# Decoder layer on one core: in the attention stage, the sum of the two output halves, its split, the output projection and the residual addition move one step later, and the first group of transposes moves to directly behind the scores

## The chip, the cores and the metric

The kernel runs on one core of one Trainium2 chip. The metric is the device time of one execution in microseconds (us); lower is better. TensorE is called PE here, VectorE DVE, ScalarE ACT, GpSimd POOL and SyncE SP, as in the profile. Each of the five works through a queue of its own in program order, and the queues wait for each other only by semaphores that are written into the kernel by hand.

## The reference, cut to what matters

A pre-norm decoder layer on x of 4 x 512 x 512: causal attention with 32 query heads and 8 key/value heads of size 64, then a small cross attention, then a mixture of 8 experts. The change touches only the attention, which is:

```python
    q = _rope((x @ Wq.T).reshape(B, L, HQ, HD))      # B 4, L 512, HQ 32, HD 64
    k = _rope((x @ Wk.T).reshape(B, L, HKV, HD))     # HKV 8, so G = 4 query heads share one
    v = (x @ Wv.T).reshape(B, L, HKV, HD)
    attn = einsum('bkgqd,bkld->bkgql', qh, kh) * SCALE
    p = softmax(where(causal, attn, -inf), axis=-1)
    out = einsum('bkgql,bkld->bkgqd', p, vh)
    return out @ Wo.T                                # added to x
```

## The kernel before, in words

All operands of the matmuls are split into a high and a low part (`_hi`, `_lo`), each held in a reduced 32-bit type, and each product is two or three matmuls over these parts. ACT makes the high part with a copy (`act_split`), and DVE subtracts it from the source for the low part (`dve_lo`, line L422).

The attention walks over 8 groups (one key/value head each). In a group it walks over 16 steps `c`: 4 batches `b` times 4 heads `h`. A step is a slice of a software pipeline, and every engine has its own function that issues its part of step `c`: `pe_group`, `act_group`, `dve_group`, `pool_group`. The order of the calls in these four functions is the order of work; nothing else schedules it. Groups 1 to 6 are two trips through a loop with three groups in its body.

In step `c` head `n + 1` gets its scores on PE (L208, 8 matmuls), the causal mask and row maximum on DVE (`dve_masked`, L434), the exponential on ACT (`act_exp`, L313), reciprocals on DVE (`dve_recip`, L441) and its normalisation on POOL (`pool_norm`, L546). Head `d = c - 1` has its probabilities transposed on PE in three units (`pe_ptrans`, L218): unit 0 of 4 tiles, unit 1 of 4 tiles, and unit 2 of 2 tiles, which comes at the very start of the next step. Units 0 and 2 share one PSUM bank, unit 1 has another, so unit 0 of a head must wait until unit 2 of the head before was read by ACT (`pt_hi`, the copy) and DVE (`pt_lo`, the subtraction). Then head `d - 1` is multiplied with v (`pe_pv`, L235, 8 matmuls into the one bank `O_BANK`). Its result comes as two halves: ACT copies one to `o_part` (`act_opart`, tile `v_and_o`), DVE adds the other (`dve_oadd`, L487, tile `o_f`), which also frees `O_BANK` for the next `pe_pv`. After two heads the pair is split (`act_o` gives `o_hi`, `dve_o` gives `o_lo`). Once in a step PE projects one of the four row blocks of the last finished batch (`pe_wo`, L247, 6 matmuls), ACT copies this out (`act_wo`, L372), and POOL adds it to the residual (`pool_woacc`, L562).

Three of four steps also hold a projection for the next batch (`pe_proj`, L185, 12 matmuls): of v and k at h = 0, of queries at h = 1 and 2. At h = 3 there is none, only a small transpose of v (`pe_vt`, L195). I call h = 3 the short step. Rotary embedding of these takes DVE (`dve_rope_in`, L452 and L453), POOL (`pool_rope`, two operations, L537 and L539), ACT (`act_rope`) and DVE or POOL (`dve_q_lo`, L459 and L460; `pool_k_lo`, L554). Once in a group the next weights are split, too: `w2` by ACT and DVE, `w1` by ACT and POOL at `W1_SLOTS` (b = 2, h = 1, 2, 3).

Of the kernel before, what the change touches and what calls it, by code (L numbers as in the profile page):

```python
# [26 lines left out]
B, L, D = 4, 512, 512  # L27
# [71 lines left out]
def decoder_layer(nc, x, ctx, ctx_cols, mem_mask, wqkv, wo_rows, router_cols, router_b, gu_w, gu_b, down_w, down_b,  # L99
                  cos_t, sin_t, causal_t, ident_t, iota_t, out):  # L100
    stack = ExitStack()
    with stack:
# [149 lines left out]
        def pe_group(pe, g, r):  # L252
# [4 lines left out]
            for c in range(HEADS + (isinstance(g, int) and g == GROUPS - 1)):  # L257
# [9 lines left out]
                d_here = not (isinstance(g, int) and g == 0 and d < 0)  # L267
                d_begun = not (isinstance(g, int) and g == 0 and d < 1)
                d_last = not (isinstance(g, int) and g == 0 and db < 1)
                d_before_last = not (isinstance(g, int) and g == 0 and db < 2)  # L270
# [26 lines left out]
                if dh in (1, 2) and d_last:  # L297
                    if dh == 1 and db == 1:
                        pe.wait_ge(s["w2_lo_done"], 2 * g + 2)
                    pe_wo(pe, dm - 1, (db - 1) % 2, dh - 1)  # L300
                if dh == 0 and d_before_last:
                    pe_wo(pe, dm - 2, db % 2, 3)
# [71 lines left out]
        def act_group(act, g, r):  # L374

            for c in range(HEADS + (isinstance(g, int) and g == GROUPS - 1)):
# [9 lines left out]
                d_here = not (isinstance(g, int) and g == 0 and d < 0)  # L386
                d_begun = not (isinstance(g, int) and g == 0 and d < 1)
                d_last = not (isinstance(g, int) and g == 0 and db < 1)
                d_before_last = not (isinstance(g, int) and g == 0 and db < 2)
# [13 lines left out]
                if dh == 3 and d_last:  # L403
                    act_wo(act, dm - 1, 2)
                if h == 3 and next_batch:
                    act_v(act, m + 1, (b + 1) % 2)
                if d_begun:
                    act_opart(act, dn_ - 1)
                if dh in (1, 2) and d_last:
# [1260 lines left out]
```

## Time and profile before

| what | value |
|---|---|
| median of 3 runs | 1655.32 us (1653.87 to 1656.75) |
| profiled execution, its time and its span | 1654.71 us, 1653.0 us |
| busy share PE, DVE, ACT, POOL over the span | 90%, 80%, 67%, 63% |
| granted PE clock over 180 to 900 us | 1.00 |
| PE busy in 420 to 540 us | 112.66 of 120.00 us |
| DVE, ACT, POOL busy there | 98.44, 96.71, 98.39 us |

The attention takes from about 60 us to about 1065 us of the span; what follows is not changed. The profile's idle times stand in brackets behind an instruction, with what ended them.

### The profile page before, as it was taken

The numbers are of one execution on the slowest core, as the hardware profiler recorded it, in microseconds if no ns is written. First come the engines' busy times: TensorE is split into PE (matmuls) and PEld (weight loads), VectorE is DVE, ScalarE is ACT, GpSimd is POOL, SyncE is SP. The second block draws the span as 40 slices with busy tenths as digits, with TensorE's granted clock in tenths as the row PEclk, the third lists the DMA queues.
The fourth block names the chain that finished last, engine by engine and source line by source line (L and its number), as shares of the span: only waits on it lengthen the run. The fifth ranks groups of instructions, "written<-read, shape, count | busy, mean of one in ns | idle before, by whom it ended". The sixth has DMA issues, their size and how long they took to land. (4 is left out here: it accounts for less than half of the span.)

```text
span 1653.0 us, 31706 instructions
## 1 busy us (share of the span) xinstructions
PE 1487.3 (90%) x8951; PEld 1305.1 (79%) x8951; DVE 1329.5 (80%) x3470; ACT 1113.7 (67%) x2593; POOL 1049.0 (63%) x1161
## 2 busy tenths in 40 slices
PE   5799999999999999999999999698689999999994
PEld 4678888888888778878878877577479999999993
DVE  7688888888888888888888888388678998898892
ACT  3687887887887788788778878432156666666661
POOL 6668878878878878878878877556613223322321
PEclk9799999999999999999999999967589999999997
DMA  4000000000000000000000000112368878888775
GB/s 173 1 13 20 2 14 20 1 14 20 1 14 21 3 14 20 1 14 20 1 14 1 1 1 1 41 64 90 108 213 230 238 218 217 232 236 219 196 180 134
DMA packets 62033, 124.98 MB, mean 76 GB/s; under 512 B 20942, under 2 KB 21070, under 8 KB 61792
## 3 DMA queue, kind: packets, MB, share of 16 engines
q1 hardware_dynamic: 51408, 102.24, 19.5%
q0 software_dynamic: 10304, 20.59, 6.6%
q8 instruction: 77, 1.26, 0.3%
q14 instruction: 100, 0.82, 0.2%
q10 hardware_dynamic: 144, 0.07, 0.0%
HBM read 106.08 MB, written 24.71 MB: 79 GB/s over the span
## 5 line engine op out<-in xcount | busy, mean ns | idle before, releaser
L546 POOL TENSOR_SCALAR probs<-probs,row_inv 128x512 f32<-128x512 f32 (+3 forms) x512 | 303.6, 614 | 15.1 <-DVE row_inv L441 15.1
L313 ACT ACTIVATE probs<-probs,neg_max 128x512 f32<-128x512 f32 (+3 forms) x512 | 281.7, 552 | 28.5 <-DVE neg_max L434 25.6
L434 DVE CUSTOM_DVE_ANT_0 probs<-bank,causal 128x512 f32<-128x512 f32 (+3 forms) x512 | 220.5, 485 | 54.6 <-PE bank L208 53.7
L1246 POOL DMA_INDIRECT acc<-ctx_raw,idx x46 | 74.6, 1621 | 294.3 <-ACT ctx_raw L1399 280.0
L218 PE MATMUL bank<-ident,probs 128*128 128x128 f32 x1280 | 185.0, 275 | 60.1 <-DVE pt_lo L422 55.7
L422 DVE TENSOR_TENSOR pt_lo<-bank,pt_hi 128x512 fp32r<-128x512 f32 (+1 forms) x384 | 216.3, 591 | 26.2 <-ACT pt_hi L306 26.2
L218 PEld LDWEIGHTS bank<-ident,probs 128*128 128x128 f32 x1280 | 149.7, 141 | 96.8 <-DVE pt_lo L422 58.8
L537 POOL TENSOR_TENSOR rot<-rot,sin 128x512 f32<-128x512 f32 (+1 forms) x96 | 123.6, 1287 | 156.2 <-DVE rot L453 151.7
L1327 PE MATMUL bank<-xt_hi,gu_hi 128*128 128x256 f32 x736 | 208.1, 283 | 2.0 <-DVE xt_lo L422 1.5
L1327 PE MATMUL bank<-xt_hi,gu_lo 128*128 128x256 f32 x736 | 206.3, 280 | 0.0
L1327 PE MATMUL bank<-xt_lo,gu_hi 128*128 128x256 f32 x736 | 206.3, 280 | 0.0
L306 ACT ACTIVATE pt_hi<-bank 128x512 fp32r<-128x512 f32 (+1 forms) x384 | 184.9, 515 | 29.8 <-PE bank L218 26.7
L562 POOL TENSOR_TENSOR x_res<-wo_out,x_res 128x512 f32<-128x512 f32 x128 | 168.6, 1317 | 24.6 <-ACT wo_out L372 24.3
L208 PE MATMUL bank<-k_hi,q_st 128*128 128x256 f32 (+2 forms) x512 | 173.4, 349 | 2.7 <-DVE xn_lo L422 2.7
L235 PE MATMUL bank<-pt_hi,v_st 128*128 128x256 f32 (+2 forms) x512 | 170.5, 344 | 1.5 <-DVE pt_lo L422 1.5
L208 PE MATMUL bank<-k_lo,q_st 128*128 128x256 f32 (+2 forms) x512 | 157.4, 329 | 0.0
L235 PE MATMUL bank<-pt_lo,v_st 128*128 128x256 f32 (+2 forms) x512 | 155.0, 325 | 0.0
L185 PE MATMUL bank<-xn_hi,w_hi 128*128 128x512 f32 x384 | 152.8, 398 | 0.2 <-DVE rot L453 0.2
L185 PE MATMUL bank<-xn_lo,w_hi 128*128 128x512 f32 x384 | 151.5, 394 | 0.0
L185 PE MATMUL bank<-xn_hi,w_lo 128*128 128x512 f32 x384 | 151.1, 394 | 0.0
L1327 PEld LDWEIGHTS bank<-xt_hi,gu_hi 128*128 128x128 f32 x736 | 138.9, 189 | 6.0 <-issue 2.8
L1327 PEld LDWEIGHTS bank<-xt_lo,gu_hi 128*128 128x128 f32 x736 | 139.2, 189 | 3.0
(203 smaller groups left out, 4077.4 us busy)
## 6 DMA issues: line engine op xcount, KB each, us to landing
gu_raw<-in_gate_up SPq DMA_DIRECT2D x92, 512.0 KB, 4.2
dn_raw<-in_down SPq DMA_DIRECT2D x92, 256.0 KB, 3.7
w_raw<-in_wqkv SPq DMA_DIRECT2D x8, 768.0 KB, 4.5
w_raw<-in_wo_rows SPq DMA_DIRECT2D x8, 512.0 KB, 3.6
h_rows<-ln_h SPq DMA_DIRECT2D x16, 256.0 KB, 2.0
acc<-x_res SPq DMA_DIRECT2D x4, 1024.0 KB, 4.8
x_res<-in_x SPq DMA_DIRECT2D x3, 1024.0 KB, 11.3
ctx_raw<-in_ctx SPq DMA_DIRECT2D x2, 512.0 KB, 6.5
```

The source lines that it names most:

```text
L185: last = nc.tensor.matmul(PJ_BANK[:, :], w1[sp][:, c, r * P:(r + 1) * P], xn[mp][:, c, b * L:(b + 1) * L], start=first, stop=(c == DC - 1 ...
L208: last = nc.tensor.matmul(S_BANK[k][:, at:at + cols], q_st[:, h, i * P:(i + 1) * P], kk[:, kb, 0:cols], start=(a == 0), stop=(a == 1))
L218: last = nc.tensor.transpose(T_BANK[u % 2][:, k * P:(k + 1) * P], probs[:, hb, P_AT[i] + j * P:P_AT[i] + (j + 1) * P], ident[:, :])
L235: last = nc.tensor.matmul(dst, v_st[:, vb, j, :], rhs, start=(j == 0 and a == 0), stop=(j == QB - 1 and a == 1))
L306: nc.scalar.activation(dst, src, ACT.Copy).then_inc(sem_, 1)
L313: nc.scalar.activation(row, row, ACT.Exp, bias=neg_max[:, hb, i:i + 1], scale=-1.0, accum_out=row_sum[:, hb, i:i + 1]).then_inc(s["exp_don ...
L422: nc.vector.tensor_tensor(dst, src, hi.bitcast(F32), ALU.subtract).then_inc(sem_, 1)
L434: nc.vector.tensor_tensor_reduce(out=probs[:, hb, P_AT[i]:P_AT[i] + (i + 1) * P], in0=S_BANK[k][:, at:at + (i + 1) * P], in1=causal[:, (QB ...
L537: nc.gpsimd.tensor_tensor(rot[0:rows, :], rot[0:rows, :], sin[0:rows, :], ALU.mult).then_inc(s["rot_sin"], 1)
L546: nc.gpsimd.tensor_scalar(row, row, row_inv[:, hb, i:i + 1], 0.0, ALU.mult, ALU.add).then_inc(s["pnorm_done"], 1)
L562: nc.gpsimd.tensor_tensor(tile, wo_out[:, t % 2, :], tile, ALU.add).then_inc(s["woacc_done"], 1)
L1327: last = nc.tensor.matmul(GU_BANK[u % 3][:, side * TILE:(side + 1) * TILE], gu[sp_][:, ib, c, side, :], xts[mp][:, k, c, :], start=first, ...
```

## The change

`f = c - 2` is new. The sum of output halves, the split of the pair, the split of `w2`, the output projection, its copy and the residual addition now go by `f` where they went by `d = c - 1`: each is done for a head or a row block one step later. Unit 0 of the transposes, its copy and its subtraction are cut off from unit 1 and put directly behind the scores on PE. On ACT the order is now unit 2, output half, unit 0, then rotary and exponential; on DVE it is unit 2, split of the pair, sum, then the mask, then unit 0. The last group has one step more, and the tail behind it is shorter by that.

```diff
@@ pe_group
                 if more:
                     pe_scores(pe, n + 1, m if h < G - 1 else m + 1, (h + 1) % G, (b + (h == G - 1)) % 2)
+                if d_here:
+                    pe_ptrans(pe, dn_, (r + d) % 3, 0)
...
-                if dh == 3 and d_last:
-                    pe_wo(pe, dm - 1, (db - 1) % 2, 2)
+                if fh == 3 and f_last:
+                    pe_wo(pe, fm - 1, (fb - 1) % 2, 2)
                 if d_here:
-                    pe_ptrans(pe, dn_, (r + d) % 3, 0)
                     pe_ptrans(pe, dn_, (r + d) % 3, 1)
@@ act_group
                 if d_begun:
                     act_pt(act, dn_ - 1, (d + 1) % 2, 2)
+                if f_begun:
+                    act_opart(act, fn - 1)
+                if d_here:
+                    act_pt(act, dn_, d % 2, 0)
...
+                if f_begun and fh % 2 == 0:
+                    act_o(act, fn - 1, fm if fh else fm - 1, (f // 2 - 1) % 4)
                 if d_here:
-                    act_pt(act, dn_, d % 2, 0)
                     act_pt(act, dn_, d % 2, 1)
@@ dve_group
+                if d_begun:
+                    dve_pt(dve, dn_ - 1, (d + 1) % 2, 2)
+                if f_begun and fh % 2 == 1 and not (isinstance(g, int) and g == 0 and f == 1):
+                    dve_o(dve, HEADS // 2 * g + (f - 1) // 2 - 1, ((f - 1) // 2 - 1) % 4)
+                if f_begun:
+                    dve_oadd(dve, fn - 1, (f - 1) % 2, HEADS // 2 * g + (f - 1) // 2)
+                if fh == 1 and fb == 1:
+                    dve_w2(dve, g)
                 if more:
                     dve_masked(dve, n + 1, (r + c + 1) % 3)
-                if d_begun:
-                    dve_pt(dve, dn_ - 1, (d + 1) % 2, 2)
...
+                if d_here:
+                    dve_pt(dve, dn_, d % 2, 0)
...
                 if d_here:
-                    dve_pt(dve, dn_, d % 2, 0)
                     dve_pt(dve, dn_, d % 2, 1)
                 if h == 3 and next_batch:
                     dve_v(dve, m + 1, (b + 1) % 2)
-                if d_begun:
-                    dve_oadd(dve, dn_ - 1, (d - 1) % 2, HEADS // 2 * g + (d - 1) // 2)
```

DVE, the short step (h = 3), before: `pt1_lo` with 256 columns is unit 2, and the two `pt0_lo` are units 0 and 1 of the next head.

```order
L434 ISA probs,neg_max<-bank0,causal 128x512
L434 ISA neg_max 128x1
L434 ISA probs,neg_max<-bank1,causal 128x384
L434 ISA neg_max 128x1
L434 ISA probs,neg_max<-bank2,causal 128x256
L434 ISA neg_max 128x1
L434 ISA probs,neg_max<-bank2,causal 128x128
L434 ISA neg_max 128x1
L422 TENSOR_TENSOR pt1_lo<-bank3,pt1_hi 128x256
L441 RECIPROCAL row_inv<-row_sum 128x4
L422 TENSOR_TENSOR pt0_lo<-bank3,pt0_hi 128x512
L422 TENSOR_TENSOR pt0_lo<-bank4,pt0_hi 128x512
```

DVE, the same step after (lines are 10 higher there).

```order
L432 TENSOR_TENSOR pt0_lo<-bank3,pt0_hi 128x256
L432 TENSOR_TENSOR o_lo<-o_f,o_hi 128x512
L497 TENSOR_TENSOR o_f<-bank5,v_and_o 64x512
L444 ISA probs,neg_max<-bank0,causal 128x512
L444 ISA neg_max 128x1
L444 ISA probs,neg_max<-bank1,causal 128x384
L444 ISA neg_max 128x1
L444 ISA probs,neg_max<-bank2,causal 128x256
L444 ISA neg_max 128x1
L444 ISA probs,neg_max<-bank2,causal 128x128
L444 ISA neg_max 128x1
L432 TENSOR_TENSOR pt1_lo<-bank3,pt1_hi 128x512
```

Unit 2 is now ahead of the mask and not behind it, and so are a split of the pair (every second step, h = 1 and 3) and the sum of halves.

ACT, the short step, after; before, it went unit 2 (`pt_hi` with 256 columns), the four exponentials, units 0 and 1, `v_st`, `v_and_o`, `wo_out`, `o_hi`.

```order
L311 ACTIVATE pt1_hi<-bank3 128x256
L311 ACTIVATE v_and_o<-bank5 64x512
L311 ACTIVATE pt0_hi<-bank3 128x512
L318 ACTIVATE probs,row_sum<-probs,neg_max 128x512
L318 ACTIVATE probs,row_sum<-probs,neg_max 128x384
L318 ACTIVATE probs,row_sum<-probs,neg_max 128x256
L318 ACTIVATE probs,row_sum<-probs,neg_max 128x128
L311 ACTIVATE pt0_hi<-bank4 128x512
L311 ACTIVATE v_st<-bank6 128x4x64
L377 ACTIVATE wo_out<-bank7 128x512
```

The copy of the output half and of unit 0 went ahead of the exponentials; `o_hi` left this step for an even one.

PE, the short step, after: before, the 4 transposes between scores and L195 stood behind L195, in one run of 8.

```order
L218 MATMUL bank<-ident,probs 128x128 x2
L208 MATMUL bank<-k_hi,q_st 128x512
L208 MATMUL bank<-k_lo,q_st 128x512
L208 MATMUL bank<-k_hi,q_st 128x384
L208 MATMUL bank<-k_lo,q_st 128x384
L208 MATMUL bank<-k_hi,q_st 128x256
L208 MATMUL bank<-k_lo,q_st 128x256
L208 MATMUL bank<-k_hi,q_st 128x256
L208 MATMUL bank<-k_lo,q_st 128x256
L218 MATMUL bank<-ident,probs 128x128 x4
L195 MATMUL bank<-ident,v_and_o 128x64 x4
L218 MATMUL bank<-ident,probs 128x128 x4
```

In the three other steps the first x4 stands between the scores and the 12 matmuls of the projection.

## Rows read from the trace of the kernel before

**Rows 1.** Busy by stretch: one group, one plain batch, one with a further wait

```profile
core 0: us, PE busy (x) PEld busy (x) DVE busy (x) ACT busy (x) POOL busy (x), PEclk, DMA share, GB/s
513.52:546.09 32.57, 29.59 (x168) 25.35 (x168) 27.13 (x68) 25.12 (x65) 28.62 (x33) 1.00 0.08 25
420.84:450.94 30.10, 29.05 (x168) 25.36 (x168) 24.72 (x68) 24.59 (x64) 24.82 (x29) 1.00 0.01 2
388.25:513.52 125.27, 117.38 (x672) 101.44 (x672) 103.66 (x274) 100.94 (x255) 103.58 (x116) 1.00 0.04 12
```

**Rows 2.** Who waited for whom on PE, 180 to 1000 us

```profile
PE bank L218 <- DVE pt_lo L422: 39.0, 43, 1.6
```

**Rows 3.** Order of time on PE, a short step and the step behind it

```profile
447.83 0.38 PE L218 MATMUL bank<-ident,probs 128*128 128x128 f32 x2
447.97 0.47 PE L208 MATMUL bank<-k_hi,q_st 128*128 128x512 f32 x1
448.28 0.39 PE L208 MATMUL bank<-k_lo,q_st 128*128 128x512 f32 x1
...
449.43 0.46 PE L195 MATMUL bank<-ident,v_and_o 64*128 64x64 f32 x4
450.94 1.09 PE L218 MATMUL bank<-ident,probs 128*128 128x128 f32 x8 [1.05 <-DVE pt_lo L422]
451.79 0.48 PE L235 MATMUL bank<-pt_hi,v_st 128*128 128x512 f32 x1
...
453.17 0.40 PE L247 MATMUL bank<-w_hi,o_hi 128*128 128x512 f32 x1
...
454.55 0.38 PE L218 MATMUL bank<-ident,probs 128*128 128x128 f32 x2
...
456.06 0.40 PE L185 MATMUL bank<-xn_hi,w_hi 128*128 128x512 f32 x1
...
458.79 0.39 PE L247 MATMUL bank<-w_hi,o_hi 128*128 128x512 f32 x1
...
460.15 1.03 PE L218 MATMUL bank<-ident,probs 128*128 128x128 f32 x8
460.94 0.48 PE L235 MATMUL bank<-pt_hi,v_st 128*128 128x512 f32 x1
```

**Rows 4.** Order of time on DVE, the same steps

```profile
448.82 0.69 DVE L434 CUSTOM_DVE_ANT_0 probs<-bank,causal 128x512 f32<-128x512 f32 x1
...
450.47 0.42 DVE L422 TENSOR_TENSOR pt_lo<-bank,pt_hi 128x256 fp32r<-128x256 f32 x1
...
454.01 0.68 DVE L487 TENSOR_TENSOR o_f<-bank,v_and_o 64x512 f32<-64x512 f32 x1
...
457.52 0.68 DVE L422 TENSOR_TENSOR o_lo<-o_f,o_hi 128x512 fp32r<-128x512 f32 x1
```

**Rows 5.** Order of time on ACT, the same short step

```profile
448.11 0.60 ACT L372 ACTIVATE wo_out<-bank 128x512 f32<-128x512 f32 x1 [0.33 <-PE bank L247]
448.60 0.38 ACT L306 ACTIVATE pt_hi<-bank 128x256 fp32r<-128x256 f32 x1
449.55 0.72 ACT L313 ACTIVATE probs<-probs,neg_max 128x512 f32<-128x512 f32 x1 [0.57 <-DVE neg_max L434]
...
451.75 1.06 ACT L306 ACTIVATE pt_hi<-bank 128x512 fp32r<-128x512 f32 x2
452.70 0.37 ACT L306 ACTIVATE v_st<-bank 128x256 fp32r<-128x256 f32 x1
```

**Rows 6.** Order of time on POOL and DVE: same short step, and near 520 us

```profile
447.05 1.29 POOL L537 TENSOR_TENSOR rot<-rot,sin 128x512 f32<-128x512 f32 x1
448.42 1.29 POOL L539 TENSOR_TENSOR rope<-rope,rot 128x512 f32<-128x512 f32 x1
...
520.07 1.31 POOL L562 TENSOR_TENSOR x_res<-wo_out,x_res 128x512 f32<-128x512 f32 x1
520.10 3.07 DVE L422 TENSOR_TENSOR o_lo<-o_f,o_hi 128x512 fp32r<-128x512 f32 x1
521.32 1.31 POOL L469 TENSOR_TENSOR w_lo<-w_raw,w_hi 128x512 fp32r<-128x512 f32 x1
```

More of the change, by code:

```diff
@@ L252, in pe_group @@
         def pe_group(pe, g, r):
-            for c in range(HEADS + (isinstance(g, int) and g == GROUPS - 1)):
+            for c in range(HEADS + (2 if isinstance(g, int) and g == GROUPS - 1 else 0)):
                 b, h = divmod(c, G)
@@ L266, in pe_group @@
                 dn_, dm = HEADS * g + d, B * g + db
-                d_here = not (isinstance(g, int) and g == 0 and d < 0)
+                d_here = not (isinstance(g, int) and g == 0 and d < 0) and d < HEADS
                 d_begun = not (isinstance(g, int) and g == 0 and d < 1)
-                d_last = not (isinstance(g, int) and g == 0 and db < 1)
-                d_before_last = not (isinstance(g, int) and g == 0 and db < 2)
+                f = c - 2
+                fb, fh = divmod(f, G)
+                fn, fm = HEADS * g + f, B * g + fb
+                f_begun = not (isinstance(g, int) and g == 0 and f < 1)
+                f_last = not (isinstance(g, int) and g == 0 and fb < 1)
+                f_before_last = not (isinstance(g, int) and g == 0 and fb < 2)
                 if d_begun:
@@ L296, in pe_group @@
                     pe_pv(pe, dn_ - 1, dm if dh else dm - 1, (d + 1) % 2, (db if dh else db + 1) % 2)
[L297 to L298 removed]
+                if fh in (1, 2) and f_last:
+                    if fh == 1 and fb == 1:
                         pe.wait_ge(s["w2_lo_done"], 2 * g + 2)
[L300 to L302 removed]
+                    pe_wo(pe, fm - 1, (fb - 1) % 2, fh - 1)
+                if fh == 0 and f_before_last:
+                    pe_wo(pe, fm - 2, fb % 2, 3)
         def act_split(dst, src, sem_):
@@ L374, in act_group @@
         def act_group(act, g, r):
-            for c in range(HEADS + (isinstance(g, int) and g == GROUPS - 1)):
+            for c in range(HEADS + (2 if isinstance(g, int) and g == GROUPS - 1 else 0)):
                 b, h = divmod(c, G)
@@ L493, in dve_group @@
         def dve_group(dve, g, r):
-            for c in range(HEADS + (isinstance(g, int) and g == GROUPS - 1)):
+            for c in range(HEADS + (2 if isinstance(g, int) and g == GROUPS - 1 else 0)):
                 b, h = divmod(c, G)
@@ L518, in dve_group @@
                     dve_q_lo(dve, m + 1, 1, (b + 1) % 2)
-                if dh == 1 and db == 1:
-                    dve_w2(dve, g)
                 if h < 3 and next_batch:
@@ L551, in pool_k_lo @@
             wait(pool, s["pnorm_done"], 16 * m - 8)
-            wait(pool, s["woacc_done"], 4 * m - 9)
+            wait(pool, s["woacc_done"], 4 * m - 10)
             for half_ in range(2):
@@ L564, in pool_group @@
         def pool_group(pool, g, r):
-            for c in range(HEADS + (isinstance(g, int) and g == GROUPS - 1)):
+            for c in range(HEADS + (2 if isinstance(g, int) and g == GROUPS - 1 else 0)):
                 b, h = divmod(c, G)
@@ L575, in pool_group @@
                 dn_, dm = HEADS * g + d, B * g + db
-                d_here = not (isinstance(g, int) and g == 0 and d < 0)
+                d_here = not (isinstance(g, int) and g == 0 and d < 0) and d < HEADS
                 d_begun = not (isinstance(g, int) and g == 0 and d < 1)
-                d_last = not (isinstance(g, int) and g == 0 and db < 1)
-                d_before_last = not (isinstance(g, int) and g == 0 and db < 2)
+                f = c - 2
+                fb, fh = divmod(f, G)
+                fn, fm = HEADS * g + f, B * g + fb
+                f_begun = not (isinstance(g, int) and g == 0 and f < 1)
+                f_last = not (isinstance(g, int) and g == 0 and fb < 1)
+                f_before_last = not (isinstance(g, int) and g == 0 and fb < 2)
                 if h == 1 and next_batch:
```

53 lines of the change are left out of this document (26 added, 27 removed).

## The prediction

> **What bounds the kernel now.** I read the page first, then busy time by stretch, then the list of waits, then the order of time on each engine. In the attention PE is the bound, but not wholly. A group of 16 steps takes 125.27 us, with PE busy for 117.38 and DVE, ACT and POOL for 101 to 104 each [rows 1]. So PE stands idle for 7.9 us in a group, 63 us in eight; more than that the change can't win. Between 180 and 1000 us PE waited 39.0 us, in 43 waits, for the low part of the transposed probabilities [rows 2].
>
> In the short step that wait is 1.05 us: the transposes of L218 start at 450.94 [rows 3]. DVE did the mask first, from 448.82, and unit 2 behind it, from 450.47 for 0.42 us, so PE's bank came free at 450.89 [rows 4]. A plain batch of four steps has this one wait and takes 30.10 us. Two of the four batches of a group have a further one: one takes 32.57 us, and by subtraction from 125.27 the other some 32.5 [rows 1]. One of these comes from a split of the pair, o_lo, that took 3.07 us in place of 0.68, since it was issued while POOL ran two two-input operations back to back, from 520.07 to 522.63, and ended 0.54 us behind them [rows 4, 6]. The other is PE at `pe_wo` behind the split of w2.
>
> **The price list, from one plain batch.** PE: unit 2 to first score 0.14; scores to the next kind 1.38 (1.46 to L195, less a gap); 8 transposes 0.79 without a wait; PV 1.38 (451.79 to 453.17); wo 1.38; projection 2.73 [rows 3]. ACT: the copy of wo starts 0.28 behind unit 2's start on PE, unit 2's copy 0.49 behind that and takes 0.38; four exponentials 2.20 (449.55 to 451.75); one 512-column copy 0.48 to 0.53; v follows, the next thing 0.30 later [rows 5]. DVE: mask 1.65 (448.82 to 450.47), its first tile lets ACT start 0.73 later (449.55); sum of halves 0.68; o_lo 0.68 [rows 4, 5]. A semaphore costs about 0.05 between ACT, DVE and PE.
>
> **The change, part by part.** No matmul, copy or subtraction is added or taken away. The sum, its split, wo and POOL's residual keep their lengths; moving wo by a step costs PE nothing, as it is still one per step. The extra step at the end holds what was in the tail: 0, with an estimate of 1 us either way for the steps without projections around it.
>
> Cutting the run of 8 transposes in two adds a switch from transposes back to matmuls in the three long steps. The first score follows unit 2 and takes 0.31 to the second (447.97 to 448.28), where matmuls of the same size in the projection take 2.73 / 12 = 0.23. So a switch costs 0.08, and three cost 0.24 per batch [rows 3]. Bounds: 0 and 0.24.
>
> Now the queues by hand, t from unit 2's start on PE, first the short step. PE is through its scores at 1.52. ACT copies wo at 0.28, unit 2 at 0.77 to 1.15; DVE subtracts from 1.20 to 1.62; unit 0 can start at 1.67: a wait of 0.15 in place of 1.05. That is the gain, 0.90 per batch. The same 0.15 comes up at h = 1, where nothing waited before; not at h = 2, since at h = 1 wo is earlier.
>
> What is late next: DVE has o_lo and the sum ahead of the mask. o_lo is issued at about 1.54. Before, POOL ran its rotary pair in the short step from 447.05 to 449.71, t = -0.78 to 1.88 [rows 6]. In the new order DVE's rotary work in the step before is later (the sum, unit 0 and the q subtractions are ahead of it), and I put the pair's end at t = 2.15. Held until there, o_lo ends at 2.15 + 0.54 = 2.69, the sum at 3.35, and PV, which needs the sum because of the one bank for its output, starts at 3.40. PE would be ready at 1.67 + 0.40 + 0.43 + 0.40 = 2.90. That is a new wait of 0.50. Bounds: 0 if o_lo isn't held (sum by 2.85), 0.5 as here. The Trainium skill, in its page "GPSIMD Engine Reference", section "Key points", says that GpSimd shares its SBUF interfaces with VectorE and contends with DVE instructions with two SBUF inputs; o_lo is one. The 3.07 us row agrees. By the rule the wait stands for any overlap, by the row for two-input POOL operations; both give my sum here.
>
> The mask then starts at 3.30 and not at 1.0 (448.82 - 447.83). ACT begins the exponentials at 4.03, ends them at 6.23, copies unit 1 until 6.75 and v until 7.05, and only then wo. PE's next step starts at 2.90 + 0.50 + 1.38 + 1.38 = 6.16, so wo's copy is at t = 0.9 of the next step and not at 0.28; unit 2's copy at 1.4, DVE done at 2.2, unit 0 at 2.27. PE waits 0.75 there. Before, no wait stood in this place, since the exponentials ran 2 us earlier. In the step h = 0 ACT catches up: its work is some 7.2 us, the step 8.5. In long steps the late mask is hidden behind the rotary copies on ACT and 2.73 us of projection.
>
> Sum of a plain batch: 30.10 - 1.05 - about 0.2 of restart behind the stall + 0.24 (switches) + 0.15 + 0.15 + 0.50 + 0.75 = 30.64, so +0.54.
>
> The batch with w2: ACT splits w2 (two copies, 1.04) ahead of unit 2 in the short step, so unit 0 waits 1.2 and not 0.15; but PV's wait goes, since the sum is then hidden behind it. DVE does both w2 subtractions (0.7 to 0.87 each) ahead of the mask; wo waits 0.2 for them, and the wait of the next step grows from 0.75 to 2.1. I get +2.1 over a plain batch, against 2.4 before. The batch with w1: POOL's extra operation pushes the rotary pair and ACT's copies come 0.5 ahead of unit 2 at h = 3 and h = 0: short step 7.24 and not 6.2, the next one +0.5, together +1.5 against 2.4 before, as the 3.07 us of o_lo are gone.
>
> Group: 4 x 0.54 - 0.3 - 0.9 = +0.96; times 8 = +7.7. From the profiled execution's 1654.71: **1662 us**, which stands 0.4% above it and above the median of 1655.32.
>
> **The rivals.**
> (a) Forecast: the short step's wait is traded for a PV wait there and a late unit 0 in the next; slower by 4 to 16 us, 1658 to 1670 (per group 0.5 to 2, by the bounds of the switches and of the hold). Chance 0.40.
> (b) ACT keeps up, and o_lo gets in ahead of POOL: then no PV wait (0.50 less), and the lag of 0.75 in the next step shrinks to about 0.3: -0.95 per batch against (a), 4 x 8 x 0.95 = 30 us less, 1632. With one of the two alone about 1640 to 1648. For it: DVE, ACT and POOL have 21 to 24 us of slack in a group. Against: the chain unit 2, o_lo, sum, mask, exponentials, unit 1, v, wo is 6.9 us long, and the short step on PE only 5.7. Chance 0.30. This is the one on the other side; it decides when wo's copy in step h = 0 starts before t = 0.5.
> (c) The q subtractions, now behind the mask and unit 0 (t = 4.4 to 6.1 at h = 2), fall on POOL's residual addition, a two-input operation of 1.3 us, and are held. By my walk they miss it by 0.2 us. If held, the rotary pair is 1.2 later, falls wholly on o_lo in the short step, and PV waits 1.2 more: up to 4 x 8 x 1.2 = 38 us on top, 1700; in part of the batches 1680. The Trainium skill's sentence on shared interfaces speaks for it; the row of 3.07 shows its size. Chance 0.18.
> (d) Nothing to be measured: gains of the two special batches cancel the plain ones, 1652 to 1658. Chance 0.12.
>
> **How the numbers follow.** About 0.2% (3.3 us) is what a measurement of this kernel can tell from no change. Faster is (b) with the lower edge of (d) and a part of (a)'s misjudged terms: 0.32. Same: 0.14, from (d) and (a)'s lower edge. Slower: 0.54, from (a) and (c). The range leaves out 0.1 on each side: from 1638, which holds most of (b), to 1688, which holds the partial case of (c). The likeliest case's own range is 1658 to 1670.
>
> **What the profile after would show.** Right: L218 (x4) behind the scores waits about 0.15 in the short step and at h = 1; PV (L235) waits some 0.5 in the short step for the sum; L218 waits about 0.75 at h = 0 for DVE; a plain batch takes 30.6 us, a group 126.2; o_lo at 128x512 has about 1.2 us as its usual length; the mask starts 3.3 us into the short step, and ACT waits there for it. Wrong would be: wo's copy at h = 0 directly behind PE; o_lo at 0.68 throughout (b); q_st rows near 1.5 to 2 us at h = 2 (c); PE busy near 118 of 120 us. My walk rests on differences of 0.1 to 0.3 us in where POOL's pair falls, and that is what would most likely make it wrong.

## The result, and the profile after

The changed kernel takes 1656.39 us (median of 20 runs, 1652.97 to 1662.57), the kernel before 1654.58 us (20 runs, 1651.89 to 1657.19). Each ratio below is against the runs of before that were made along with the kernel; their medians lie between 1654.58 and 1655.33. Here the ratio is 1.0014 with a 95% interval of 1.0008 to 1.0021. That is 1.8 us slower. The interval leaves out 1, so the loss is real, but it is about half of the 3.3 us that the prediction took as the least to be told from no change, and a quarter of the 7.7 us forecast. In the profiled executions the last matmul of the attention ends at 1065.03 us and before at 1063.72, so 1.3 us are lost there; the rest of the program, which is the same, took 591.07 against 589.28.

Busy time by stretch in the changed kernel, from one L195 to the next: the batch with w1, a plain batch, the two batches over which the split of w2 is spread, a group. It answers to [rows 1].

```profile
core 0: us, PE busy (x) PEld busy (x) DVE busy (x) ACT busy (x) POOL busy (x), PEclk, DMA share, GB/s
385.54:416.99 31.45, 29.84 (x170) 25.38 (x169) 26.06 (x69) 25.34 (x63) 27.87 (x31) 1.00 0.08 26
416.99:447.39 30.40, 29.67 (x169) 25.38 (x169) 26.13 (x68) 24.83 (x62) 25.36 (x29) 1.00 0.01 2
447.39:478.77 31.38, 29.66 (x170) 25.39 (x169) 26.10 (x68) 25.87 (x64) 26.43 (x30) 1.00 0.00 1
478.77:511.20 32.43, 30.03 (x170) 25.36 (x169) 27.35 (x71) 25.76 (x64) 26.40 (x29) 1.00 0.06 18
385.54:511.20 125.66, 119.21 (x674) 101.50 (x673) 105.64 (x275) 101.80 (x253) 106.07 (x116) 1.00 0.04 12
```

The plain batch went from 30.10 to 30.40 us, the group from 125.27 to 125.66. PE idles less (0.73 us in the plain batch, 1.05 before), yet the batch is longer: PE is busy for 29.67 us where it was for 29.05. A group before had two plain batches, now it has one: w2 is split one step later, so its first wait on PE stands ahead of an L195 and its others behind it. That first wait, in the short step, is 1.33 us:

```profile
478.18 0.66 PE L218 MATMUL bank<-ident,probs 128*128 128x128 f32 x4 [1.33 <-DVE pt_lo L432]
```

The list of waits on PE between 180 and 1000 us, against [rows 2], has more and shorter waits of about the same sum:

```profile
PE bank L218 <- DVE pt_lo L432: 41.0, 56, 1.7
```

PE in order of time, the short step and the scores of the step behind it (the same place of the program as [rows 3]):

```profile
444.79 0.38 PE L218 MATMUL bank<-ident,probs 128*128 128x128 f32 x2
...
446.80 0.66 PE L218 MATMUL bank<-ident,probs 128*128 128x128 f32 x4 [0.34 <-DVE pt_lo L432]
...
447.78 0.65 PE L218 MATMUL bank<-ident,probs 128*128 128x128 f32 x4
448.28 0.47 PE L235 MATMUL bank<-pt_hi,v_st 128*128 128x512 f32 x1
...
451.03 0.38 PE L218 MATMUL bank<-ident,probs 128*128 128x128 f32 x2
...
453.09 0.66 PE L218 MATMUL bank<-ident,probs 128*128 128x128 f32 x4 [0.39 <-DVE pt_lo L432]
453.50 0.48 PE L185 MATMUL bank<-xn_hi,w_hi 128*128 128x512 f32 x1
...
456.35 0.60 PE L218 MATMUL bank<-ident,probs 128*128 128x128 f32 x4
```

The wait of 1.05 has become 0.34 in the short step and 0.39 at h = 0. PV (L235) at 448.28 has no wait at all. DVE and POOL there, to hold against [rows 4, 6]:

```profile
446.67 0.68 DVE L432 TENSOR_TENSOR o_lo<-o_f,o_hi 128x512 fp32r<-128x512 f32 x1
447.45 0.68 DVE L497 TENSOR_TENSOR o_f<-bank,v_and_o 64x512 f32<-64x512 f32 x1
448.06 0.67 DVE L444 CUSTOM_DVE_ANT_0 probs<-bank,causal 128x512 f32<-128x512 f32 x1
...
445.31 1.30 POOL L552 TENSOR_TENSOR rot<-rot,sin 128x512 f32<-128x512 f32 x1 [0.32 <-DVE rot L463]
446.69 1.79 POOL L554 TENSOR_TENSOR rope<-rope,rot 128x512 f32<-128x512 f32 x1
```

POOL's pair lies at t = 0.52 to 3.69 from unit 2's start at 444.79, right on o_lo, as feared. But between its two operations POOL is free for 0.08 us (446.61 to 446.69), and o_lo starts in just this gap: it takes 0.68, and POOL's addition 1.79 in place of 1.29. In the plain batch's other split, at h = 1, o_lo does start beside a running POOL addition (430.50) and takes 1.68, but no wait on PE follows from it. ACT, against [rows 5]:

```profile
445.45 0.58 ACT L377 ACTIVATE wo_out<-bank 128x512 f32<-128x512 f32 x1
445.92 0.37 ACT L311 ACTIVATE pt_hi<-bank 128x256 fp32r<-128x256 f32 x1
...
451.72 0.58 ACT L377 ACTIVATE wo_out<-bank 128x512 f32<-128x512 f32 x1
```

The copy of wo comes 0.66 behind unit 2 in the short step, where it came at 0.28, and 0.69 at h = 0.

**A ring without PE.** What sets the 30.40? Follow the other engines through a plain batch:

```profile
428.84 1.29 POOL L552 TENSOR_TENSOR rot<-rot,sin 64x512 f32<-64x512 f32 x1 [4.17 <-DVE rot L463]
...
433.99 1.29 POOL L577 TENSOR_TENSOR x_res<-wo_out,x_res 128x512 f32<-128x512 f32 x1
435.36 2.65 POOL L569 TENSOR_TENSOR k_lo<-rope,k_hi 64x512 fp32r<-64x512 f32 x2
438.17 1.29 POOL L552 TENSOR_TENSOR rot<-rot,sin 128x512 f32<-128x512 f32 x1 [0.16 <-POOL k_lo L569]
439.53 1.29 POOL L554 TENSOR_TENSOR rope<-rope,rot 128x512 f32<-128x512 f32 x1
...
459.15 1.29 POOL L552 TENSOR_TENSOR rot<-rot,sin 64x512 f32<-64x512 f32 x1 [4.08 <-DVE rot L463]
```

POOL works without a pause of more than 0.2 us from 428.84 to 440.80. ACT waits for its end to make the high part of the queries (440.94), then does exponentials, `o_hi`, unit 1, wo (445.45) and unit 2. DVE goes on with unit 2, o_lo, sum and mask (448.06). ACT waits for the mask, then does its exponentials, unit 1, v, wo and unit 2 (to 452.58) and `o_part`. DVE waits for `o_part`, then does sum, mask, unit 0, the subtractions of the queries and the rotary input, and with that releases POOL at 459.15. One turn is 459.15 - 428.84 = 30.31 us, the length of the batch; at each link the instruction starts on the end of the one named before it, and none of them is a wait for PE. So I had a second theory, that this ring, and not PE, sets the plain batch.

### The profile page after: what moved, and what is told of

Same layout as the page of the kernel before. It is cut to its first block and busy times, and to the rows that moved or that the text cites. A ratio compares the mean times of both kernels' runs of the same rounds, so it can differ in the third digit from the quotient of the medians.

```text
span 1656.1 us, 31706 instructions
## 1 busy us (share of the span) xinstructions
PE 1502.3 (91%) x8951; PEld 1307.8 (79%) x8951; DVE 1345.6 (81%) x3470; ACT 1119.9 (68%) x2593; POOL 1070.5 (65%) x1161
## 5 line engine op out<-in xcount | busy, mean ns | idle before, releaser
L432 DVE TENSOR_TENSOR pt_lo<-bank,pt_hi 128x512 fp32r<-128x512 f32 (+1 forms) x384 | 229.8, 599 | 87.5 <-ACT pt_hi L311 79.8
L311 ACT ACTIVATE pt_hi<-bank 128x512 fp32r<-128x512 f32 (+1 forms) x384 | 199.6, 521 | 98.5 <-PE bank L218 96.9
L218 PE MATMUL bank<-ident,probs 128*128 128x128 f32 x1280 | 208.5, 278 | 58.2 <-DVE pt_lo L432 56.6
L218 PEld LDWEIGHTS bank<-ident,probs 128*128 128x128 f32 x1280 | 150.0, 140 | 104.1 <-DVE pt_lo L432 52.4
L577 POOL TENSOR_TENSOR x_res<-wo_out,x_res 128x512 f32<-128x512 f32 x128 | 178.7, 1396 | 14.9 <-ACT wo_out L377 14.6
L235 PE MATMUL bank<-pt_hi,v_st 128*128 128x256 f32 (+2 forms) x512 | 172.1, 347 | 2.0 <-DVE o_f L497 1.9
L185 PE MATMUL bank<-xn_hi,w_hi 128*128 128x512 f32 x384 | 161.2, 420 | 0.3 <-DVE rot L463 0.3
L235 PE MATMUL bank<-pt_lo,v_st 128*128 128x256 f32 (+2 forms) x512 | 156.7, 327 | 0.0
```

The source lines that it names most:

```text
L185: last = nc.tensor.matmul(PJ_BANK[:, :], w1[sp][:, c, r * P:(r + 1) * P], xn[mp][:, c, b * L:(b + 1) * L], start=first, stop=(c == DC - 1 ...
L218: last = nc.tensor.transpose(T_BANK[u % 2][:, k * P:(k + 1) * P], probs[:, hb, P_AT[i] + j * P:P_AT[i] + (j + 1) * P], ident[:, :])
L235: last = nc.tensor.matmul(dst, v_st[:, vb, j, :], rhs, start=(j == 0 and a == 0), stop=(j == QB - 1 and a == 1))
L311: nc.scalar.activation(dst, src, ACT.Copy).then_inc(sem_, 1)
L432: nc.vector.tensor_tensor(dst, src, hi.bitcast(F32), ALU.subtract).then_inc(sem_, 1)
L577: nc.gpsimd.tensor_tensor(tile, wo_out[:, t % 2, :], tile, ALU.add).then_inc(s["woacc_done"], 1)
```

## The experiments

All changes are against the changed kernel where nothing else is said. "Plain" is the plain batch from one L195 to the next, "end" the end of the last L247, "rest" the span behind it; these three are of the profiled execution. "wo" is the output projection, "residual" POOL's residual addition.

| kernel | median us | ratio to before, 95% | plain | end | rest |
|---|---|---|---|---|---|
| before | 1654.58 | 1 | 30.12 | 1063.72 | 589.28 |
| after | 1656.39 | 1.0014 [1.0008, 1.0021] | 30.40 | 1065.03 | 591.07 |
| x1 unit 0 early alone, on before | 1717.38 | 1.0389 [1.0366, 1.0411] | 32.24 | 1123.82 | 590.18 |
| x2 unit 0 early at h = 3 only | 1674.77 | 1.0126 [1.0106, 1.0146] | 30.96 | 1079.47 | 588.83 |
| x3 split of the pair earlier | 1658.21 | 1.0024 [1.001, 1.0038] | 29.95 | 1063.74 | 592.16 |
| x4 copy of wo behind unit 2 | 1655.51 | 1.0002 [0.9991, 1.0014] | 30.38 | 1061.97 | 593.73 |
| x5 residual later | 1652.06 | 0.9984 [0.9975, 0.9992] | 30.21 | 1058.75 | 591.95 |
| x6 extra POOL work in the ring | 1700.31 | 1.0275 [1.0259, 1.029] | 31.50 | 1108.59 | 591.01 |
| x7 the same outside of it | 1663.11 | 1.0058 [1.0045, 1.0071] | 30.39 | 1069.86 | 588.84 |
| x8 o_lo a little later | 1661.63 | 1.0052 [1.0037, 1.0067] | 30.39 or 31.52 | 1066.66 | 591.64 |
| x9 shift by a step alone | 1681.42 | 1.0158 [1.0143, 1.0172] | 31.53 | 1086.87 | 591.13 |
| x10 x9 and residual later | 1673.07 | 1.0103 [1.0088, 1.0119] | 30.96 | 1080.55 | 591.65 |
| x11 x3 and x5 | 1655.01 | 0.9994 [0.9983, 1.0005] | 29.82 | 1059.34 | 594.36 |
| x12 x3, x4 and x5 | 1642.79 | 0.9919 [0.9906, 0.9931] | 29.81 | 1053.13 | 589.67 |

### The failing term: is o_lo held, and what does that cost?

**x8.** A small memset stands ahead of the split in the short step, to push it out of the gap.

```diff
+                if h == 3 and next_batch:
+                    nc.vector.memset(tiny[:, 0:16], 0.0)
                 if f_begun and fh % 2 == 1 and not (...):
                     dve_o(dve, ...)
```

> The changed kernel with a small memset on VectorE (128x16) ahead of the subtraction that makes the low half of the output (o_lo) in the step h=3, so that this subtraction comes some 0.06 us or more later and misses the gap of 0.08 us between GpSimd's rotary product and addition. Theory hold (a two-input subtraction of VectorE that starts beside a running two-input op of GpSimd is held to its end): o_lo takes 1.5 to 2.4 us instead of 0.68 in each batch, the PV matmuls of the short step wait or the ring gets longer by 0.8 to 1.3 us, total 1675 to 1700 us, as far as the forecast of 1662 and beyond. Rival (no hold, or the hold is hidden there): o_lo 0.7 to 0.9 us or hidden, total 1654 to 1660 us.

Of the seven short steps in front of a plain batch between 160 and 930 us, three have o_lo at 1.77 or 1.78 us, and their batches take 31.43 to 31.52 us; the other four have it at 0.67. Two of these places in the trace of x8, in the first o_lo held, in the second not (DVE, POOL, and PE's PV):

```profile
417.09 1.77 DVE L433 TENSOR_TENSOR o_lo<-o_f,o_hi 128x512 fp32r<-128x512 f32 x1
417.05 1.26 POOL L557 TENSOR_TENSOR rope<-rope,rot 128x512 f32<-128x512 f32 x1
419.80 0.47 PE L236 MATMUL bank<-pt_hi,v_st 128*128 128x512 f32 x1 [0.95 <-DVE o_f L498]
...
543.84 0.67 DVE L433 TENSOR_TENSOR o_lo<-o_f,o_hi 128x512 fp32r<-128x512 f32 x1
543.83 1.81 POOL L557 TENSOR_TENSOR rope<-rope,rot 128x512 f32<-128x512 f32 x1
545.44 0.47 PE L236 MATMUL bank<-pt_hi,v_st 128*128 128x512 f32 x1
```

And the stretches, the first with o_lo held at its start, the second with o_lo not held:

```profile
417.80:449.32 31.52, 29.83 (x170) 25.40 (x169) 27.22 (x70) 24.82 (x62) 25.25 (x29) 1.00 0.01 2
672.84:703.23 30.39, 29.68 (x169) 25.39 (x169) 26.14 (x69) 24.81 (x62) 25.37 (x29) 1.00 0.01 2
```

The hold exists, it makes PV wait 0.95 us, and it lengthens the batch by 1.13 us. Where DVE's operation starts 0.04 us after POOL's, DVE pays 1.1; where the two start within 0.02, POOL pays 0.5. The step between the two is sharp: of all short steps in x8, o_lo at 0.03 us behind POOL's start was held and at 0.023 not.

How long a held o_lo lasts follows from POOL's operation. In the 14 traces between 160 and 1050 us, a POOL operation was already running at the start of o_lo 584 times. In 558 of these o_lo ended 0.53 to 0.72 us behind that operation's end, be it a TENSOR_TENSOR or a TENSOR_SCALAR; in 24 a further POOL operation followed at once and came first too, as in the 3.07 us of [rows 6]. If all eight plain batches were held, 8 x 1.13 = 9 us would come on top of 1656.4, an estimate of 1665. The expected 1675 and more was too much: in only three of the seven places did the small memset move o_lo far enough to be held.

### The two parts of the change apart

**x1.** Only unit 0 is moved to directly behind the scores, on all engines, and DVE's unit 2 ahead of the mask; the sum, its split and wo stay in their step.

```diff
@@ on the kernel before; pe_group, act_group and dve_group alike
                 if more:
                     pe_scores(...)
+                if d_here:
+                    pe_ptrans(pe, dn_, (r + d) % 3, 0)
...
-                    pe_ptrans(pe, dn_, (r + d) % 3, 0)
                     pe_ptrans(pe, dn_, (r + d) % 3, 1)
```

> The kernel before, with only one part of the change: unit 0 directly behind the scores on all three engines and unit 2 ahead of the mask on DVE; sum, split, projection and residual where they were. My theory: the short step's wait falls from 1.05 to about 0.3 us, but in each other step unit 0 now has only the 1.4 us of scores to hide copy and subtraction of unit 2, with wo_out (and every second step o_hi) ahead of them on ACT, so it waits 0.15 at h = 1 and about 0.7 at h = 0 and h = 2, and the switches cost 0.24: a plain batch about 30.8 us (30.10 before), in all 1660 to 1675 us. Rival, the transposes alone bring the gain and the shift by one step is what costs it: a plain batch below 29.6 us, 1640 us or less. Rival, PE's waits are only moved since another engine bounds the batch: 1655 us within 3.

It is far slower than any theory had it. In its plain batch PE waits for unit 0 in each of the four steps, 2.34 us together, most at h = 0, where ACT first waits for the sum to make `o_hi` and only then copies unit 2:

```profile
445.90 0.63 ACT L307 ACTIVATE o_hi<-o_f 128x512 fp32r<-128x512 f32 x1 [0.30 <-DVE o_f L489]
...
447.31 0.66 PE L218 MATMUL bank<-ident,probs 128*128 128x128 f32 x4 [1.35 <-DVE pt_lo L424]
```

**x9.** The other part alone: the shift by one step, with unit 0 beside unit 1 and DVE's mask ahead of unit 2, as before.

```diff
@@ dve_group; pe_group and act_group have unit 0 back beside unit 1 too
+                if more:
+                    dve_masked(dve, n + 1, (r + c + 1) % 3)
                 if d_begun:
                     dve_pt(dve, dn_ - 1, (d + 1) % 2, 2)
...
-                if more:
-                    dve_masked(dve, n + 1, (r + c + 1) % 3)
-                if d_here:
-                    dve_pt(dve, dn_, d % 2, 0)
```

> Only one part of the change: the sum of the output halves, its split, the projection and the residual one step later as in the changed kernel, but unit 0 of the transposes beside unit 1 as before, on all engines, and VectorE's mask ahead of the subtraction of unit 2. With it the two parts and their sum are known: transposes alone gave 1717, both 1656. Theory parts that need each other: the shift alone takes o_hi and the sum off the chain of the short step and costs no switches (TensorE's work 29.06 us in a plain batch as before), but GpSimd, ScalarE and VectorE close their ring, so the plain batch is 29.6 to 30.4 us, total 1640 to 1660 us. Rival (the shift is the harmful part that the early unit mends): plain batch over 31 us, total over 1670 us.

The rival's numbers came, 1681 us and 31.53 us. Its short step, on DVE and PE:

```profile
455.04 0.42 DVE L432 TENSOR_TENSOR pt_lo<-bank,pt_hi 128x256 fp32r<-128x256 f32 x1
...
456.16 0.68 DVE L497 TENSOR_TENSOR o_f<-bank,v_and_o 64x512 f32<-64x512 f32 x1
...
455.51 1.09 PE L218 MATMUL bank<-ident,probs 128*128 128x128 f32 x8 [1.05 <-DVE pt_lo L432]
456.99 0.47 PE L235 MATMUL bank<-pt_hi,v_st 128*128 128x512 f32 x1 [0.38 <-DVE o_f L497]
```

The old wait of 1.05 stays, since unit 2 still stands behind the mask, and the sum, now behind unit 2, brings the PV wait that I had forecast for the whole change. The two waits are 1.43 of the batch's 31.53 us, where before it was 1.05 of 30.12; most of the rest is PE's busy time, 29.91 where it was 29.06, though no switch between kinds of matmul was added. So each part alone costs (+62 and +26 us on the medians), and together they cost 1.8: by the rows, the shift takes the sum off the chain to unit 0, and the early unit 2 takes the mask off the chain to the sum.

x9 has one more thing to show, at h = 1 (DVE, then POOL):

```profile
439.20 2.04 DVE L432 TENSOR_TENSOR o_lo<-o_f,o_hi 128x512 fp32r<-128x512 f32 x1
...
437.36 2.07 POOL L561 TENSOR_SCALAR probs<-probs,row_inv 128x512 f32<-128x512 f32 x4
439.38 1.31 POOL L577 TENSOR_TENSOR x_res<-wo_out,x_res 128x512 f32<-128x512 f32 x1
```

Here o_lo starts 0.18 us ahead of POOL's addition and is held all the same, to 0.55 us behind the addition's end, and so it is in 18 places of this trace. POOL's normalisation was still running when o_lo started. Being ahead of the next POOL operation is not enough; POOL has to be idle.

**x2.** Unit 0 early only at h = 3, where the wait was; beside unit 1 elsewhere, which saves the switches.

```diff
-                if d_here:
+                if d_here and h == 3:
                     pe_ptrans(pe, dn_, (r + d) % 3, 0)
...
+                if d_here and h != 3:
+                    pe_ptrans(pe, dn_, (r + d) % 3, 0)
```

> The changed kernel with unit 0 early in the short step alone; in the three long steps it goes back to unit 1 on PE, ACT and DVE. My theory: the waits of 0.39 at h = 0 and those at h = 1 vanish behind the projection, and so do three switches of 0.08, so a plain batch takes 29.5 to 29.7 us (30.40 in the changed kernel, 30.10 before), in all about 1630 us (1625 to 1640). Rival, unit 0 early in the long steps is what keeps ACT and DVE on time, or these two bound the batch: no gain, 1652 to 1660 us, with the wait moved to unit 2 or PV.

A miss: 18 us slower than the changed kernel. In the long steps ACT and DVE now treat unit 0 behind the late exponentials, and unit 2 of the following step needs the same bank:

```profile
434.19 0.44 PE L218 MATMUL bank<-ident,probs 128*128 128x128 f32 x2 [0.51 <-DVE pt_lo L436]
```

The waits of this kind before and behind it are 0.72 and 0.70. The switches that x2 saves are worth less; how little stands in the part on why the prediction was wrong.

### Is there a ring?

**x6 and x7.** One more POOL addition of 128x480 elements per batch, whose result nobody reads: in x6 between k_lo and the rotary product of h = 1, in x7 at the end of h = 3.

```diff
@@ x6
                 if h == 1 and next_batch:
                     pool_k_lo(pool, m + 1, (b + 1) % 2)
+                    nc.gpsimd.tensor_tensor(spare[:, :], cos[:, 0:480], sin[:, 0:480], ALU.add)
@@ x7, behind pool_woacc
+                if h == 3 and next_batch:
+                    nc.gpsimd.tensor_tensor(spare[:, :], cos[:, 0:480], sin[:, 0:480], ALU.add)
```

> The changed kernel with an added GpSimd addition of 128x480 elements from two inputs (about 1.2 us by the durations of the neighbouring ones) in h=1 of each batch, between k_lo and the second rotary product. Nothing reads its result. Theory ring: it lies in the ring, so each of 32 batches takes 1.2 us longer, total +35 to +42 us, about 1691 to 1699 us. Rival (ring not closed; TensorE's side sets the batch): the op falls in time that GpSimd waits anyway later in the batch, total +0 to +10 us.

> The same added GpSimd addition of 128x480 elements, but at the end of h=3 of each batch, in front of GpSimd's wait of 4 us for the next rotary input. Theory ring: there GpSimd has slack, total unchanged within 3 us (1654 to 1660 us). A theory by which GpSimd's busy share sets the batch expects +35 to +42 us, as in the other place.

x6, POOL's new operation, then the plain batch:

```profile
450.56 1.22 POOL L603 TENSOR_TENSOR spare<-cos,sin 128x480 bf16<-128x480 f32 x1
...
429.47:460.97 31.50, 29.84 (x169) 25.42 (x168) 26.12 (x68) 24.82 (x62) 26.53 (x30) 1.00 0.01 2
```

x7, the batch with w1 and a plain batch:

```profile
386.82:419.40 32.58, 30.09 (x170) 25.45 (x169) 27.36 (x69) 25.32 (x63) 29.01 (x32) 1.00 0.08 25
419.40:449.79 30.39, 29.66 (x169) 25.37 (x168) 26.13 (x68) 24.80 (x62) 26.55 (x30) 1.00 0.01 2
```

The same operation lengthens the plain batch by 1.10 us in one place and not at all in the other: POOL's load is equal in both (26.53 and 26.55), so it is the place that counts. One turn of POOL's rotary work is now 31.42 us (441.31 to 472.73), 1.11 more. The two runs show that the place is on the path that closes the batch; that no wait for PE lies on this path rests on the rows. x6 costs 44 us in all and not 35: most batches, not only the plain ones, grew by about 1.1 us, and five grew by 2.2 to 3.4.

In x7 only the batch with w1 grew (32.58 from L195 to L195, 31.45 without the operation). There `w_lo` follows at once, and the subtraction of the queries is issued beside the two, in DVE's and POOL's order of time:

```profile
396.40 2.46 DVE L470 TENSOR_TENSOR q_st<-rope,q_st 64x512 fp32r<-64x512 f32 x1
...
395.85 1.22 POOL L611 TENSOR_TENSOR spare<-cos,sin 128x480 bf16<-128x480 f32 x1
397.03 1.29 POOL L480 TENSOR_TENSOR w_lo<-w_raw,w_hi 128x512 fp32r<-128x512 f32 x1
```

It is held to the end of both, 2.46 us in place of 1.28 in the changed kernel, which is the whole growth. This is the mechanism of rival (c), with its price, in a place where it can happen.

**x5.** One POOL residual addition out of the ring.

```diff
@@ pool_group, behind pool_rope
+                if h == 1:
+                    e = c - 3
+                    eb, em = e // G, B * g + e // G
+                    if not (isinstance(g, int) and g == 0 and eb < 1):
+                        pool_woacc(pool, em - 1, (eb - 1) % B, 1)
...
-                if fh and f_last:
+                if fh and f_last and h != 0:
```

> The changed kernel with one edit: GpSimd's residual addition that stood at the end of the step h=0 (1.37 us) is moved behind the second rotary addition of h=1, so it no longer stands between the norm of h=0 and the subtraction for k_lo. Theory ring (the plain batch of 30.4 us is closed by a chain of GpSimd, ScalarE and VectorE instructions in which TensorE does not take part): the ring loses 1.37 us, the plain batch goes from 30.40 to 29.3 to 29.7 us, where TensorE's own work stops it (its waits in a plain batch are about 1 us together), TensorE's waits nearly vanish, total 1625 to 1640 us. Rival (the transposes and their subtractions on TensorE's side set the batch): plain batch 30.4 as before, total 1654 to 1659 us.

The direction is right and the size wrong: 4.3 us faster than the changed kernel, where 16 and more were expected. In its plain batch PE is busy for nearly all of the time:

```profile
412.73:442.94 30.21, 29.73 (x169) 25.38 (x168) 26.36 (x69) 24.92 (x62) 25.39 (x29) 1.00 0.01 2
```

With the ring 1.3 us shorter the batch loses 0.19 us and meets the next bound, PE's own 29.7 us with one wait of 0.38. Both limits lay within 0.2 us of each other in the plain batch.

**x3 and x4.** x3 moves the split of the pair one step earlier, ahead of unit 1's subtraction, so that o_lo leaves the ring; x4 moves ACT's copy of wo behind the copy of unit 2 in the step after it.

```diff
@@ x3, dve_group
-                if f_begun and fh % 2 == 1 and not (...):
-                    dve_o(dve, HEADS // 2 * g + (f - 1) // 2 - 1, ...)
...
+                if f_begun and fh % 2 == 0:
+                    dve_o(dve, HEADS // 2 * g + f // 2 - 1, (f // 2 - 1) % 4)
                 if d_here:
                     dve_pt(dve, dn_, d % 2, 1)
@@ x4, act_group, behind unit 2
+                if eh and not (isinstance(g, int) and g == 0 and eb < 1):
+                    act_wo(act, em - 1, eh - 1)
```

> The changed kernel with the low part of the output pair (o_lo) made one step earlier, in the step in which ACT makes o_hi, ahead of the subtraction of unit 1, so that it no longer stands ahead of the mask in the short step. My theory, the mask that comes late by o_lo and the sum is what makes ACT late at h = 0: the mask starts 0.6 us earlier in the short step, the wait at h = 0 (0.39) goes, that of unit 0 in the short step grows by about 0.15, a plain batch 30.0 to 30.1 us, in all 1643 to 1648 us. Rival, ACT is late for its own work and not for the mask: the wait at h = 0 stays, 1655 us within 3.

> The changed kernel with ACT's copy of the projected rows (wo_out) behind the copy of unit 2 of the next step and not ahead of it; POOL's residual addition follows it. My theory, unit 0 waits for a chain wo_out copy, unit 2 copy, subtraction that is longer than the scores: it becomes 0.3 to 0.5 us shorter in every step, the waits of unit 0 at h = 3 and h = 0 (0.34 and 0.39) nearly vanish in plain batches, a plain batch about 29.6 to 29.9 us, in all 1630 to 1640 us. Rival, the wait follows from the late exponentials and the order of the two copies changes nothing: 30.3 us, 1655 us within 3.

Both missed the expected totals, and both fit the ring: x3 takes an instruction out of it (plain 29.95), x4 only exchanges two of its links (30.38), and PE's waits there are 0.55 and 0.29. That fit is an argument from one number each; what the gain in x3's plain batch is given back to in its total was not followed.

**x10.** The edit of x5 on x9.

> The shift alone as in x9, and GpSimd's residual addition of h=0 moved behind the second rotary addition of h=1 as in x5. Theory ring: if the ring bounds x9, this takes up to 1.4 us off each plain batch, down to TensorE's own work plus small waits, 29.2 to 29.8 us, total 1625 to 1648 us. Rival (TensorE waits for the unit that is transposed last in the short step, as in the kernel before): no change against x9 within 0.3 us a batch.

The plain batch falls from 31.53 to 30.96 and the total by 8 us. That is more than the 0.3 us of the rival and far less than the ring theory gave, so in x9 both the ring and PE's waits take part; it was not resolved further.

### Towards a faster version

**x11** joins x3 and x5, **x12** joins x3, x4 and x5.

> The changed kernel with the residual addition later (x5: plain batch 30.21) and VectorE's split of the output one step earlier (x3: 29.95). Theory: the two act on different things, the ring and the wait of unit 0, so the plain batch is 29.7 to 29.9 us, close to TensorE's own work of some 29.4 to 29.7; the attention ends 6 to 9 us earlier than in the changed kernel, of which 1 to 5 us show in the total: 1645 to 1652 us. Rival (both act on the same wait): no better than x5, 1650 to 1655 us.

> As x11, and ScalarE's copy of the projection's result behind its copy of unit 2 in the following step (x4). Theory: in x4 this moved waits without ending them since the ring stood; with the ring shorter, TensorE gains up to 0.2 us a batch more, 1640 to 1650 us. Rival: TensorE is at its own work already, total as x11 within 3 us.

x12 is faster than both kernels, by 12.5 us against before. That lies in the range expected by the theory and outside that of the rival. Against x11 it is 12.2 us faster; of the 10.9 between the two profiled spans 6.2 lie in the attention and 4.7 in the rest, which is the same program. Near 454 us in x12, DVE and POOL:

```profile
454.42 0.65 DVE L433 TENSOR_TENSOR o_lo<-o_f,o_hi 128x512 fp32r<-128x512 f32 x1
...
454.52 1.71 POOL L553 TENSOR_TENSOR rot<-rot,sin 64x512 f32<-64x512 f32 x1 [3.90 <-DVE rot L464]
```

Now o_lo starts 0.1 us ahead of an idle POOL and is held in one place alone: between 180 and 1000 us its 52 instances take 694 ns on average, against 1212 in x11 and 1073 in the changed kernel. The batch behind the plain one takes 29.90 us in x12 and 31.45 in x11. The batch with w1 is longer instead, 32.24 against 31.00, with a wait of 1.03 ahead of the scores of one step. That the gain comes from o_lo is not shown: the move of the copy of wo also takes unit 2's copy earlier, and no run has parted the two.

## Why the prediction was wrong

By steps of the plain batch, from one unit 2 on PE (L218 x2) to the next, in us; the five plain batches measured in each kernel agree within 0.07, but for the short step before, which is 6.71 to 6.83:

| step | before | after | change | forecast |
|---|---|---|---|---|
| h = 0 | 7.77 | 8.43 | +0.66 | 0.75 + 0.08 |
| h = 1 | 7.82 | 7.95 | +0.13 | 0.15 + 0.08 |
| h = 2 | 7.80 | 7.79 | -0.01 | 0.08 |
| h = 3, the short step | 6.72 | 6.24 | -0.48 | -1.05 - 0.2 + 0.15 + 0.50 |
| sum | 30.11 | 30.41 | +0.30 | +0.54 |

- **The step that failed** is "Held until there, o_lo ends at 2.15 + 0.54 = 2.69, ... That is a new wait of 0.50". The pair did lie on o_lo, later even than put there (end at t = 3.69), but o_lo started at t = 1.88 in the 0.08 us between its two operations, and the wait is 0. The rule and its 0.54 hold: in x8 o_lo ends 0.55 us behind POOL's addition. But as the pair ended later than 2.15, a hold would have cost more than 0.50, namely 0.95. The walk treated the pair as one block. That o_lo fell into the gap in the short steps of the changed kernel is luck, by a few hundredths of a microsecond. The forecast sign "about 1.2 us as its usual length" nearly came, 1.07 on average, but from the splits at h = 1, where PE doesn't wait for it. The Trainium skill, "GPSIMD Engine Reference", section "Key points", names contention between GpSimd and VectorE instructions with two SBUF inputs. Trace and x8 agree, with 1.77 us held and 0.67 not, but they show that it goes by whether POOL's operation was already running when DVE's started, not by overlap as such.
- **0.75 at h = 0**: 0.39 in the profile. The copy of wo was at t = 0.69 and not at 0.9, because PV did not wait and the chain of the short step began earlier. This follows from the step above. **0.15 in the short step**: 0.34, since the copy of wo was at 0.66 there as well and not at 0.28; that ACT is late when it enters the short step was missed. **0.15 at h = 1**: no wait is listed there, yet the step grew by 0.13.
- **The switches** were put at 0.24 and cost nothing. The step h = 2 has a switch more and no wait, and it is as long as before: the projection takes 2.83 us where it took 2.73, and the two runs of 4 transposes 0.35 each where the run of 8 took 0.79. x9, which adds no switch, has PE busy for 29.91 us.
- **The restart** was counted once, as 0.2 to be won, and each new wait has its own. Scores last 1.38, so unit 0 would stand at 446.31 and stands at 446.80, with a bracket of 0.34: the step loses 0.15 more than its bracket says. It is the same at h = 0 (452.55, 453.09 and 0.39), and the transposes behind a wait take 0.41 us and not 0.35. This, and not the switches, is most of the 0.62 us by which PE's busy time grew. So the waits came 0.82 too high (0.73 for 1.55) and the rest 0.58 too low, which makes the 0.24 between 30.64 and 30.40: two errors that partly cancel.
- **The special batches**: forecast were 2.1 and 1.5 over a plain batch, 3.6 together. The profile has 1.05, 0.98 and 2.03 over 30.40, 4.06 together. The 0.98 and a part of the 2.03 are w2's, the rest is w1's, whose waits also stand on both sides of an L195; how the 2.03 divides is left open. They were put 0.46 too low.
- **The sum**: a group grew by 4 x 0.30 for the plain part and fell by 0.81 for the special ones (4.87 before), +0.39 where +0.96 was forecast. From the first L195 to the end of the attention the six middle groups together lost 1.8 us, the first and the last group gained 3.8, and the stretch behind the last L195 grew from 47.3 to 50.0 us, where the forecast put 0, with 1 us either way, for the extra step; the first L195 is 0.6 us later. Together that is the 1.3 us of the profiles.
- **What it didn't see** is the ring. Taking 0.3 us off PE's waits could not shorten the batch, since POOL, ACT and DVE close it in 30.31 us by themselves. A walk along PE's waits alone finds neither this nor x12.
- Rival (b) named both facts, o_lo ahead of POOL and less lag at h = 0, and still forecast 1632: it took (a)'s sum less these two waits, with the restarts in it 0.58 too low and no ring. Its own sign, the copy of wo at h = 0 before t = 0.5, did not come. The result is that of (d), and in part for its reason: the special batches gave back 0.81 of the 1.20 us that a group lost by the plain part.

## What to carry to other kernels

Before a wait on the busiest engine is traded, follow the other engines once around the loop: if their chain returns in the loop's own time, the wait is only where the ring shows, and an operation added in two places of one queue tells ring from slack. Moves that each cost time alone can be neutral or a gain together, so try them joined before they are dropped. Where a DVE operation with two SBUF inputs lies beside POOL's work, put it where POOL is idle when it starts, since a few hundredths of a microsecond decide who pays. And price a wait by the length of the whole step, not by its bracket alone: here each of the two new waits cost 0.15 us more than was listed.

## What the runs showed of the hardware

- A 128x512 subtraction from SBUF takes 0.68 us on DVE when it starts in a gap of 0.08 us of POOL's work and 1.77 when it comes 0.04 us after POOL's next one (x8). In the first case POOL's operation takes 1.79 to 1.81 in place of 1.29. A held one ends 0.53 to 0.72 us behind the end of the POOL operation that was running, and in x9 and in [rows 6] behind the end of the POOL operation after it.
- A switch between transposes and 512-column matmuls on PE costs nothing over the step (7.80 us before and 7.79 after at h = 2). The waits of 0.34 and 0.39 each cost about 0.15 us more than their brackets.
- Time gained in the attention is partly given back or not, by no rule that these runs show. The rest of the program, with the same instructions, took 588.8 to 594.4 us in the 14 profiled executions, with a mean granted clock of PE of 0.88 or 0.89 in twelve of them and of 0.87 in x4 and x11, at 593.73 and 594.36 us. Before and x4 from the end of the attention on:

```profile
1063.72:1653.00 589.28, 522.08 (x3511) 476.47 (x3511) 472.22 (x1191) 294.43 (x553) 207.15 (x209) 0.89 0.66 183
...
1061.97:1655.70 593.73, 529.05 (x3512) 486.29 (x3511) 472.76 (x1191) 294.76 (x553) 207.14 (x209) 0.87 0.65 182
```

PE is busy for 7 us more with the same matmuls at a lower granted clock. So x4 and x11, which end the attention 1.8 and 4.4 us earlier than before, show nothing of it in their totals. Why the clock falls in some kernels and not in others stays open.
